# Preparing eight experts' weights in five rounds of a convolution-and-attention pipeline instead of eight

## The chip, the cores and the metric

One core of one Trainium2 chip runs the whole program. The metric is the device time of one execution in microseconds (us). The engines are TensorE (PE; PEld is its weight load), VectorE (DVE), ScalarE (ACT), GpSimd (POOL) and SyncE (SP), which only issues DMAs.

## The reference

Sixteen images of 128 channels by 16x16 go through three parts, and each part is added to its input:

```
x = x + conv(group_norm(x))         # per-image 7x7 depthwise filters, made from the image itself:
                                    # softmax keys, filters = query @ keys, 1x1 conv, layer norm, relu, 1x1 conv
t = tokens(x)                       # 256 tokens of 128 per image
t = t + attention(layer_norm(t))    # q = tanh(z); softmax(q q^T / sqrt(128)) z
t = t + moe(layer_norm(t))          # 8 experts, the best 2 per token:
   h = x @ w1[e] + b1[e]
   y = (silu(h @ wg[e] + bg[e]) * (h @ wv[e] + bv[e])) @ w2[e] + b2[e]
```

There is nothing nonlinear between `w1` and `wg`, `wv`. So the kernel multiplies them once per expert: `w1[e] @ [wg[e] | wv[e]]`, a 128x512 matrix, with the bias row added, and later sends token rows through that product.

## The kernel before, in words

The work has two halves. The first is a software pipeline over 8 pairs of images. In round i (0 to 8, loop `for i in range(rounds)` of each engine's program) seven stages work on seven pairs: n = i (group norm statistics), a = i-1 (keys and transposes of the normalised pair), b = i-2 (filters), c = i-3 (convolution by spectra, and the layer norm of its result), d = i-4 (attention), e = i-5 (router), f = i-6 (sending rows to `rows_dram`). So round 0 has only n, round 1 has n and a, round 2 has b as well, and round 6 is the first with all seven. Round 8 has no n. After round 8 a tail, written out by hand, finishes the last pairs. The second half runs 71 blocks of 128 token rows through the experts, starting at about 201 us.

Each engine executes its own list in the order written; semaphores tie them. Inside a round TensorE does: transposes of the new pair (L1204, they wait for `g_done`, which ScalarE gives with `gbuf` L627), keys (L1209), the first 1x1 conv (L1145), the filter spectrum of c (L1163), transposes for attention (L1140), filter mean (L1149), the spectrum of the features (L1095), router transposes (L1103), scores (L1170), router (L1110), filter variance (L1153), **one expert's weights (`expert_weights`, L1188)**, transposes of the keys' softmax (L1277), the group average of the means (L1283, it waits for `gn_mv_done` of VectorE L929), the convolution's inverse transform (`image`, L1178), ranks, the group average of the squares (L1296), raw filters (L1303), attention (L1132), and the last 1x1 conv (`filter_of`, L1158). `keep_busy` (L1090) puts 128x256 matmuls without use into gaps of the early rounds.

One expert x costs, by engine: VectorE `weight_differences` (L678, L679: makes `w1d`, at the end of the round before), TensorE two 128x512 matmuls into `bank_d0` (L1188), VectorE `weight_bias` (L686, adds the bias to row 0 of the bank), ScalarE the copy to `w_high` (L600 or L614), VectorE `low_part` (L692: bank minus `w_high` to `w_low`). Rounds 1 to 8 do expert i-1 each. `wgv`, `w1t` and `bg_row` are double-buffered by x % 2, and SyncE's `reload_w(x)` waits for `wmul_psum` of expert x-2 before it loads.

GpSimd computes inverse roots (L440 for the filters, L446 for group norm, L450 and L459 for the two layer norms) and issues indirect DMAs of rows (L429), all in one queue: in a round from 6 on, two rows' worth (4 DMAs) stand between L440 and L446.

Of the kernel before, what the change touches and what calls it, by code (L numbers as in the profile page):

```python
# [32 lines left out]
ALU = mybir.AluOpType  # L33
# [93 lines left out]
def build(nc, a_in, out):  # L127
# [9 lines left out]
    with ctx:  # L137
# [202 lines left out]

        expert_rounds = list(range(1, EXPERTS + 1))

        def experts_through(i):

            return sum(r <= i for r in expert_rounds)

        def expert_in(i):
            return experts_through(i) - 1 if i in expert_rounds else None

# [5 lines left out]
        with nc.Block() as block:  # L355

            @block.sync
            def _(sp):
# [35 lines left out]
                for p in range(2, PAIRS):  # L394

                    sp.wait_ge(g_done, p - 1)
                    load_x(p)
                    if p < EXPERTS - 1:
                        reload_w(p)

                    if p < 2 + PAIRS // 2:
                        sp.dma_start(xt[:, 2 * p - 4:2 * p - 2], a_in["xt"][:, 2 * p - 4:2 * p - 2]).then_inc(ld_xt[p % 2], 16)
                reload_w(EXPERTS - 1)
                sp.dma_start(w2_all[:, :], a_in["w2"]).then_inc(ld_w2, 16)
# [99 lines left out]
            def _(act):  # L504
# [45 lines left out]
                def rest_spectrum(b):  # L550
                    act.wait_ge(ghat_psum, 2 * b + 2)
                    act.activation(ghat[0:BOTH, b % 2, 2, :], bank_s1[0:BOTH, 0:2 * C], ACT.Copy).then_inc(ghat_done, 1)

                def tanh_of(d):
# [13 lines left out]
                for i in range(rounds):  # L568
                    n, a, b, c, d, e, _ = stages(i)
                    x = expert_in(i)  # L570
                    if a is not None:

                        act.wait_ge(gt_psum, a + 1)
                        after(act, fraw_psum, a - 1)
                        after(act, ghat_psum, 2 * (a - 1))
                        act.activation(gt[:, a % 2, :, :].rearrange("p h c -> p (h c)"), bank_t[:, :], ACT.Copy).then_inc(gt_done, 1)
                    if b is not None:
                        first_conv(b)
# [18 lines left out]
                    if x is not None and b is None and a is not None:  # L597

                        act.wait_ge(wbias_done, x + 1)
                        act.activation(w_high[:, x * 2 * HID:(x + 1) * 2 * HID], bank_d0[:, :], ACT.Copy).then_inc(whigh_done, 1)  # L600
                    if d is not None:
# [9 lines left out]
                    if x is not None and b is not None and a is not None:  # L611

                        act.wait_ge(wbias_done, x + 1)
                        act.activation(w_high[:, x * 2 * HID:(x + 1) * 2 * HID], bank_d0[:, :], ACT.Copy).then_inc(whigh_done, 1)  # L614
                    if a is not None:
# [39 lines left out]
            def _(dve):  # L655
# [25 lines left out]

                def weight_bias(x):

                    dve.wait_ge(wmul_psum, x + 1)
                    dve.wait_ge(ld_bg[x % 2], 16 * (x // 2 + 1))
                    dve.tensor_tensor(bank_d0[0:1, :], bank_d0[0:1, :], bg_row[:, x % 2, :], ALU.add).then_inc(wbias_done, 1)  # L686

                def low_part(x):
# [3 lines left out]
                    dve.tensor_tensor(w_low[:, columns], bank_d0[:, :], w_high[:, columns], ALU.subtract).then_inc(wlow_done, 1)  # L692

# [179 lines left out]
                for i in range(rounds):  # L873
                    n, a, b, c, d, e, _ = stages(i)
                    x = expert_in(i)
                    if i == 1:

                        dve.wait_ge(ld_c1, 32)
                        dve.tensor_copy(before[:, :], cst("before")).then_inc(const_ready, 1)
                        dve.wait_ge(ld_router, 32)  # L880
                        dve.tensor_tensor(router_d[:, :], router_w, router_0[:, :], ALU.subtract).then_inc(router_sub, 1)
                        dve.wait_ge(router_sub, 1)
                        dve.tensor_copy(router_d[0:1, :], router_b[:, :]).then_inc(router_done, 1)
                        experts["triangle"](dve)
                        image_statistics(n)
                    if b is not None:
                        centred(b)
# [13 lines left out]
                    if x is not None and b is None and a is not None:  # L901
                        weight_bias(x)
                    if c is not None:
# [34 lines left out]
                    if x is not None and a is not None:  # L938
                        if b is not None:
                            weight_bias(x)  # L940
                        low_part(x)
                    if n is not None:
# [140 lines left out]
            def _(pe):  # L1083
# [97 lines left out]

                def expert_weights(i, x):

                    pe.wait_ge(wdiff_done, x + 1)
                    after(pe, prod_done, through(i, CC))
                    after(pe, wlow_done, x)
                    for h in range(2):
                        last = pe.matmul(bank_d0[:, :], w1d[:, h, :], wgv[:, x % 2, h, :], start=(h == 0), stop=(h == 1))  # L1188
                    last.then_inc(wmul_psum, 1)

                for i in range(rounds):
                    n, a, b, c, d, e, _ = stages(i)
                    x = expert_in(i)
                    if a is not None:
# [16 lines left out]
                    if x is not None and b is None and a is not None:  # L1211
                        expert_weights(i, x)
                    if b is not None:
# [49 lines left out]
                    if b is not None:  # L1263

                        if b < 2:
                            keep_busy(bank_o[:, 0:2 * P], 3)
                        after(pe, logits_done, through(i, E))
                        filter_square(b)
                    if x is not None and b is not None and a is not None:
                        expert_weights(i, x)  # L1270
                    if a is not None:
# [582 lines left out]
```

## Time and profile before

| what | value |
|---|---|
| median of 3 runs | 332.0 us (331.98 to 333.33) |
| the profiled execution: its own time | 332.57 us |
| its span, first to last instruction | 330.6 us |
| mean granted TensorE clock | 0.969 of full |
| busy over the span | PE 90%, PEld 72%, DVE 70%, ACT 44%, POOL 50% |
| chain that ended last, by engine | PE 65%, DVE 16%, issue 6%, POOL 4%, DMA 3%, ACT 3% |

The span begins at the first instruction; 2.0 us of the execution's time lie around it. A time in the text as "at 104.45" counts from the start of the span. "Records" of TensorE are halves of a matmul here: each fp32 matmul shows as two.

### The profile page before, as it was taken

What the parts mean: (1) busy time and instruction counts of PE and PEld (TensorE: products, weight loads), DVE (VectorE), ACT (ScalarE), POOL (GpSimd) and SP (SyncE); (2) the same over time, 40 slices, a digit from 0 to 9 for tenths busy, and PEclk for the clock granted to TensorE, in tenths of its full rate; (3) what the DMA queues carried; (4) which work ended last, traced back from release to release, by engine and by line L of the source; (5) the groups of instructions that cost most, each with busy time, mean ns of one, the idle gap of its engine ahead of it and who ended that gap; (6) DMA issues with size and microseconds to landing.
All of it is one profiled execution on the core that took longest, in us unless ns stands there. A gap on an engine that the chain in (4) does not pass through costs nothing.

```text
span 330.6 us, 7141 instructions
## 1 busy us (share of the span) xinstructions
PE 296.0 (90%) x1733; PEld 236.5 (72%) x1733; DVE 232.8 (70%) x1012; ACT 144.5 (44%) x465; POOL 164.7 (50%) x187
## 2 busy tenths in 40 slices
PE   0889999999999999999998986999999999999910
PEld 0557777688777778778876764876888888888810
DVE  2424375679788797877889795688666676767883
ACT  1344343625237352461420424555566666666600
POOL 3000002021163746636748765667777777676650
PEclk9979999999999999999999998799999999999985
DMA  6751423050211811001101113334433333335937
GB/s 189 281 171 45 133 76 102 4 168 5 80 48 34 285 39 35 16 24 36 34 25 50 44 41 93 99 98 108 113 92 104 89 105 108 97 84 153 353 131 250
DMA packets 29920, 33.39 MB, mean 101 GB/s; under 512 B 5064, under 2 KB 23836, under 8 KB 29626
## 3 DMA queue, kind: packets, MB, share of 16 engines
q1 hardware_dynamic: 24608, 23.64, 24.3%
q0 software_dynamic: 4352, 8.60, 7.6%
q10 hardware_dynamic: 922, 0.71, 0.7%
q8 instruction: 16, 0.26, 0.4%
q14 instruction: 22, 0.18, 0.2%
HBM read 21.69 MB, written 11.68 MB: 101 GB/s over the span
## 4 chain that ended last, share of the span: by engine, by line
PE 65%; DVE 16%; issue 6%; POOL 4%; DMA 3%; ACT 3%; DVEq 1%; POOLq 0%; SPq 0%; ACTq 0%
PE bank L1784 7%; PE bank L1178 6%; PE bank L1095 6%; PE bank L1188 4%; PE bank L1759 4%; PE bank L1764 4%; PE bank L1760 4%; PE bank L1773 4%; PE bank L1163 3%; PE bank L1170 3%; PE bank L1090 3%; POOL rows_dram L429 3%; PE bank L1754 2%; DVE ys L1699 2%; PE bank L1132 2%
## 5 line engine op out<-in xcount | busy, mean ns | idle before, releaser
L1492 POOL DMA_INDIRECT moe_dram<-ys,xs x71 | 70.0, 987 | 29.0 <-issue 19.5
L429 POOL DMA_INDIRECT rows_dram<-row,slot x56 | 55.6, 993 | 24.6 <-issue 13.5
L1784 PE MATMUL bank<-w_all,gatedt 128*128 x284 | 44.1, 278 | 0.1
L1580 ACT ACTIVATE silu<-bank 128x256 f32<-128x256 f32 x71 | 27.2, 383 | 33.3 <-PE bank L1764 32.9
L1699 DVE SCALAR_TENSOR_TENSOR ys<-b_all,xs,bank 128x128 f32<-128x128 f32 x71 | 24.7, 348 | 23.0 <-issue 20.5
L1716 DVE SCALAR_TENSOR_TENSOR gated<-bank,xs,silu 128x256 f32<-128x256 f32 x71 | 34.2, 482 | 7.4 <-ACT silu L1580 3.4
L1784 PEld LDWEIGHTS bank<-w_all,gatedt 128*128 128x128 f32 x284 | 37.7, 193 | 0.3 <-issue 0.3
L1759 PE MATMUL bank<-w_high,x_high 128*128 x71 | 34.8, 491 | 2.6 <-ACT x_high L1567 2.6
L440 POOL TENSOR_TENSOR frstd<-fvar,minus_half 128x2 f32<-128x2 f32 x7 | 4.9, 706 | 52.4 <-DVE fvar L802 52.4
L1764 PE MATMUL bank<-w_high,x_low 128*128 x71 | 29.5, 415 | 0.4
L1178 PE MATMUL bank<-zhat,const 121*128 121x256 f32 (+1 forms) x128 | 29.6, 383 | 0.1
L1760 PE MATMUL bank<-w_low,x_high 128*128 x71 | 28.4, 400 | 0.0
L1773 PE MATMUL bank<-const,gated 128*128 128x128 f32 x142 | 27.9, 278 | 0.6 <-DVE gated L1716 0.6
L1571 ACT ACTIVATE gatedt<-bank 128x256 f32<-128x256 f32 x71 | 26.9, 379 | 1.2 <-PE bank L1773 1.1
L1773 PEld LDWEIGHTS bank<-const,gated 128*128 128x128 f32 x142 | 19.6, 142 | 9.5 <-DVE gated L1716 2.2
L1178 PEld LDWEIGHTS bank<-zhat,const 121*128 121x128 f32 (+1 forms) x128 | 23.6, 189 | 3.7 <-issue 0.5
L1567 ACT ACTIVATE x_high<-bank 128x128 fp32r<-128x128 f32 x71 | 19.7, 277 | 10.5 <-PE bank L1754 3.6
L1090 PE MATMUL bank<-const 128*128 128x256 f32 x82 | 23.5, 416 | 0.0
L1095 PE MATMUL bank<-gt,const 128*121 128x256 f32 (+1 forms) x96 | 22.8, 385 | 0.0
L1690 DVE TENSOR_TENSOR x_low<-bank,x_high 128x128 fp32r<-128x128 f32 x71 | 20.3, 286 | 3.3 <-ACT x_high L1567 3.2
L446 POOL TENSOR_TENSOR gn_rstd<-gn_var,minus_half 128x2 f32<-128x2 f32 x8 | 5.7, 715 | 32.1 <-DVE gn_var L966 32.1
L1764 PEld LDWEIGHTS bank<-w_high,x_low 128*128 128x128 f32 x71 | 13.6, 191 | 8.5 <-DVE x_low L1690 2.9
(203 smaller groups left out, 623.2 us busy)
## 6 DMA issues: line engine op xcount, KB each, us to landing
xs<-rows_dram SPq DMA_DIRECT2D x71, 66.0 KB, 1.9
xc<-in_x SPq DMA_DIRECT2D x8, 256.0 KB, 3.1
wgv<-in_wg SPq DMA_DIRECT2D x8, 256.0 KB, 2.8
wgv<-in_wv SPq DMA_DIRECT2D x8, 256.0 KB, 3.1
xt<-in_xt SPq DMA_DIRECT2D x4, 512.0 KB, 4.9
xt<-moe_dram SPq DMA_DIRECT2D x8, 256.0 KB, 4.5
moe_dram<-ys,xs POOLq DMA_INDIRECT x71, 2.3
const<-in_const SPq DMA_DIRECT2D x1, 1123.0 KB, 9.6
```

The source lines that it names most:

```text
L429: pool.indirect_dma_start(rows_dram, bass.IndirectOffsetOnAxis(ap=slot[:, f % 2, 2 * t + k:2 * t + k + 1], axis=0), row[:, f % 2, t, k, :] ...
L1090: pe.matmul(bank, ident, const[:, 0:2 * P], start=True, stop=True)
L1095: last = pe.matmul(bank_s[r // 2][0:tile_rows[r], r % 2 * 2 * C:(r % 2 + 1) * 2 * C], fwd[:, h, tile_cols[r]], gt[:, b % 2, h, :], start=( ...
L1178: last = pe.matmul(bank_o[:, h * 2 * C:(h + 1) * 2 * C], inv[0:tile_rows[r], r, h * P:(h + 1) * P], zhat[0:tile_rows[r], r, :], start=(r = ...
L1492: pool.indirect_dma_start(moe_dram, bass.IndirectOffsetOnAxis(ap=xs[:, u, C + 1:C + 2].bitcast(U32), axis=0), ys[:, u, :], None, bounds_ch ...
L1699: dve.scalar_tensor_tensor(ys[:, u, :], b2_all[:, bass.ds(e * C, C)], xs[:, u, C:C + 1], bank_y[j % 2][:, 0:C], ALU.mult, ALU.add).then_in ...
L1716: dve.scalar_tensor_tensor(gated[:, j % 2, :], bank_h[j % 2][:, HID:2 * HID], xs[:, j % U, C:C + 1], silu[:, j % 2, :], ALU.mult, ALU.mult ...
L1759: pe.matmul(bank_h[j % 2][:, :], x_high[:, j % 2, :], w_high[:, bass.ds(e * (2 * HID), 2 * HID)], start=True, stop=False)
L1760: pe.matmul(bank_h[j % 2][:, :], x_high[:, j % 2, :], w_low[:, bass.ds(e * (2 * HID), 2 * HID)], start=False, stop=False)
L1764: pe.matmul(bank_h[j % 2][:, :], x_low[:, j % 2, :], w_high[:, bass.ds(e * (2 * HID), 2 * HID)], start=False, stop=True).then_inc(S["h_psu ...
L1773: last = pe.transpose(bank_g[:, h * P:(h + 1) * P], gated[:, j % 2, h * P:(h + 1) * P], ident)
L1784: last = pe.matmul(bank_y[j % 2][:, 0:C], gatedt[:, j % 2, h * P:(h + 1) * P], w2_all[:, bass.ds(e * (2 * C) + h * C, C)], start=(h == 0), ...
```

## The change

Experts are no longer one per round. `middle_expert` says which expert is made in the old place of a round (0, 2, 4, 6, 7 in rounds 1 to 5), `late_expert` which one is made as a second one at the end of TensorE's round (1, 3, 5 in rounds 1 to 3), into `bank_o`. Rounds 6, 7 and 8 make none. The late one's bias, high copy and low part come at the start of the next round; the differences of the late expert follow `low_part` of the middle one, those of the next middle expert follow `low_part` of the late one. The loads are issued in the order in which the buffers come free. Of `keep_busy` ahead of the transposes, the counts (3, 2, 2, 4) become (3, 0, 0, 0).

```diff
-        expert_rounds = list(range(1, EXPERTS + 1))
+        middle_expert = {1: 0, 2: 2, 3: 4, 4: 6, 5: 7}
+        late_expert = {1: 1, 2: 3, 3: 5}
 SyncE:
-                    if p < EXPERTS - 1:
-                        reload_w(p)
+                    for x in {2: (2,), 3: (3, 4), 4: (5, 6), 5: (7,)}.get(p, ()):
+                        reload_w(x)
...
-                reload_w(EXPERTS - 1)
 ScalarE, after the copy to gt and before first_conv:
+                    if late_in(i - 1) is not None:
+                        high_copy(late_in(i - 1), bank_o)
 VectorE, first in the round:
+                    late = late_in(i - 1)
+                    if late is not None:
+                        weight_bias(late, bank_o)
 VectorE, after kshift (L900) and before products:
+                    if late is not None:
+                        low_part(late, bank_o)
+                        if x is not None:
+                            weight_differences(x)
 VectorE, in the middle, before gn_dev (L945):
-                        low_part(x)
+                        low_part(x, bank_d0)
+                        if late_in(i) is not None:
+                            weight_differences(late_in(i))
 VectorE, end of the round:
-                    if expert_in(i + 1) is not None:
+                    if late_in(i) is None and expert_in(i + 1) is not None:
                         weight_differences(expert_in(i + 1))
 TensorE:
-                            keep_busy(bank_t[:, 0:2 * P], (3, 2, 2, 4)[a])
+                            keep_busy(bank_t[:, 0:2 * P], (3, 0, 0, 0)[a])
...
                         if b == 0:
-                            keep_busy(bank_o[:, 0:2 * P], 1)
+                            keep_busy(bank_d1[:, 2 * P:4 * P], 1)
...
                         if b < 2:
+                            pe.wait_ge(wlow_done, late_in(i - 1) + 1)
                             keep_busy(bank_o[:, 0:2 * P], 3)
...
+                        if late_in(i - 1) is not None:
+                            pe.wait_ge(wlow_done, late_in(i - 1) + 1)
                         image(c)
...
                         filter_of(b)
+                    if late_in(i) is not None:
+                        expert_weights(i, late_in(i), bank_o)
```

## Rows read from the trace of the kernel before

**Rows 1.** Window of round 6: PE, PEld, DVE, ACT, POOL busy; clock; DMA share, GB/s.

```profile
92.95:113.50 20.55, 19.93 (x118) 15.94 (x118) 17.20 (x93) 9.16 (x31) 11.74 (x12) 1.00 0.38 111
```

**Rows 2.** The chain that ended last, round 6: start us, us, what.

```profile
103.16 0.20 DVE logits L730
...
103.79 1.82 PE bank L1188 x4
...
105.95 3.58 PE bank L1178 x16
```

**Rows 3.** Timeline of VectorE in rounds 6 and 7: start, duration, line [idle before].

```profile
98.11 1.27 DVE L723 TENSOR_SCALAR row<-t,ln_mv,ln_rstd 128x127 f32<-128x127 f32 x4 [0.31 <-POOL ln_rstd L459]
...
104.45 0.24 DVE L929 BATCH_NORM_AGGREGATE gn_mv<-gn_raw 128x2 f32<-128x6 f32 x2
...
112.06 0.16 DVE L975 SCALAR_TENSOR_TENSOR gn_bias<-gn_mean,gn_rstd 128x2 f32<-128x2 f32 x1
```

**Rows 4.** Timeline of POOL in rounds 6 and 8 and the tail.

```profile
105.16 0.72 POOL L440 TENSOR_TENSOR frstd<-fvar,minus_half 128x2 f32<-128x2 f32 x1 [4.54 <-DVE fvar L802]
...
109.95 0.95 POOL L429 DMA_INDIRECT rows_dram<-row,slot  x1 [0.30 <-issue]
110.92 0.73 POOL L446 TENSOR_TENSOR gn_rstd<-gn_var,minus_half 128x2 f32<-128x2 f32 x1
...
153.11 1.04 POOL L450 TENSOR_TENSOR ln_rstd<-ln_var,minus_half 128x4 f32<-128x4 f32 x1 [1.21 <-DVE ln_var L669]
...
172.28 1.03 POOL L429 DMA_INDIRECT rows_dram<-row,slot  x1 [3.88 <-DVE slot L789]
```

**Rows 5.** Timeline of VectorE, one pair of weight differences, start to start.

```profile
11.17 0.17 DVE L678 COPY w1d<-b1c 128x2 f32<-128x2 f32 x1 [0.93 <-DMA w1t<-in_w1t]
...
11.58 0.22 DVE L879 CAST before<-const 128x128 bf16<-128x128 f32 x1
```

**Rows 6.** Timeline of TensorE from the end of round 1 into round 2.

```profile
18.21 0.38 PE L1296 MATMUL bank<-gn_e,const 128*128 128x2 f32 x2 [0.57 <-DVE gn_e L953]
18.46 1.08 PE L1303 MATMUL bank<-pt,gt 128*128 128x64 f32 x8
19.38 1.74 PE L1090 MATMUL bank<-const 128*128 128x256 f32 x4
20.95 1.12 PE L1204 MATMUL bank<-const,gbuf 128*128 128x128 f32 x4
...
24.28 0.38 PE L1149 MATMUL bank<-fsum,const 128*128 128x2 f32 x2 [0.31 <-ACT f L534]
24.53 2.83 PE L1095 MATMUL bank<-gt,const 128*121 128x256 f32 x12
```

**Rows 7.** Windows around the low clock of round 1 (columns as in rows 1).

```profile
14.50:15.00 0.50, 0.50 (x2) 0.19 (x1) 0.00 (x0) 0.22 (x2) 0.00 (x0) 1.00 0.08 26
...
19.50:20.00 0.50, 0.50 (x3) 0.44 (x3) 0.39 (x3) 0.42 (x2) 0.08 (x1) 0.66 0.89 295
...
23.00:23.50 0.50, 0.50 (x5) 0.45 (x4) 0.00 (x0) 0.00 (x0) 0.00 (x0) 0.93 0.03 8
```

**Rows 8.** Timeline of TensorE, ends of rounds 2 and 3.

```profile
35.01 1.13 PE L1090 MATMUL bank<-const 128*128 128x256 f32 x4
36.26 0.66 PE L1204 MATMUL bank<-const,gbuf 128*128 128x128 f32 x4
...
51.52 1.99 PE L1090 MATMUL bank<-const 128*128 128x256 f32 x8
53.47 0.66 PE L1204 MATMUL bank<-const,gbuf 128*128 128x128 f32 x4
```

**Rows 9.** Timelines of ScalarE (round 3) and VectorE (rounds 3 and 4).

```profile
38.41 0.20 ACT L534 ACTIVATION_READ_ACCUMULATOR f<-bank,small 128x1 f32 x1
...
44.17 0.16 DVE L912 RECIPROCAL krec<-ktot 128x1 f32<-128x1 f32 x1 [0.92 <-ACT kexp L589]
...
64.86 0.69 DVE L686 TENSOR_TENSOR bank<-bank,bg_row 1x512 f32<-1x512 f32 x1 [1.34 <-PE bank L1188]
```

More of the change, by code:

```diff
@@ L339, in build, with late_in @@
         CC = 3
-        expert_rounds = list(range(1, EXPERTS + 1))
+        middle_expert = {1: 0, 2: 2, 3: 4, 4: 6, 5: 7}
+        late_expert = {1: 1, 2: 3, 3: 5}
         def experts_through(i):
-            return sum(r <= i for r in expert_rounds)
+            return max([x + 1 for r, x in middle_expert.items() if r <= i], default=0)
         def expert_in(i):
-            return experts_through(i) - 1 if i in expert_rounds else None
+            return middle_expert.get(i)
+        def late_in(i):
+            return late_expert.get(i)
         def after(eng, semaphore, count):
@@ L552, in rest_spectrum, with high_copy @@
                     act.activation(ghat[0:BOTH, b % 2, 2, :], bank_s1[0:BOTH, 0:2 * C], ACT.Copy).then_inc(ghat_done, 1)
+                def high_copy(x, bank):
+                    act.wait_ge(wbias_done, x + 1)
+                    act.activation(w_high[:, x * 2 * HID:(x + 1) * 2 * HID], bank[:, :], ACT.Copy).then_inc(whigh_done, 1)
                 def tanh_of(d):
@@ L597, in _ @@
                     if x is not None and b is None and a is not None:
-                        act.wait_ge(wbias_done, x + 1)
-                        act.activation(w_high[:, x * 2 * HID:(x + 1) * 2 * HID], bank_d0[:, :], ACT.Copy).then_inc(whigh_done, 1)
+                        high_copy(x, bank_d0)
                     if d is not None:
@@ L611, in _ @@
                     if x is not None and b is not None and a is not None:
-                        act.wait_ge(wbias_done, x + 1)
-                        act.activation(w_high[:, x * 2 * HID:(x + 1) * 2 * HID], bank_d0[:, :], ACT.Copy).then_inc(whigh_done, 1)
+                        high_copy(x, bank_d0)
                     if a is not None:
@@ L680, in weight_differences, with weight_bias, low_part @@
                                       w1t[:, x % 2, :, 0:1].broadcast_to([P, 2, C - 1]), ALU.subtract).then_inc(wdiff_done, 1)
-                def weight_bias(x):
+                def weight_bias(x, bank):
                     dve.wait_ge(wmul_psum, x + 1)
                     dve.wait_ge(ld_bg[x % 2], 16 * (x // 2 + 1))
-                    dve.tensor_tensor(bank_d0[0:1, :], bank_d0[0:1, :], bg_row[:, x % 2, :], ALU.add).then_inc(wbias_done, 1)
-                def low_part(x):
+                    dve.tensor_tensor(bank[0:1, :], bank[0:1, :], bg_row[:, x % 2, :], ALU.add).then_inc(wbias_done, 1)
+                def low_part(x, bank):
                     columns = slice(x * 2 * HID, (x + 1) * 2 * HID)
                     dve.wait_ge(whigh_done, x + 1)
-                    dve.tensor_tensor(w_low[:, columns], bank_d0[:, :], w_high[:, columns], ALU.subtract).then_inc(wlow_done, 1)
+                    dve.tensor_tensor(w_low[:, columns], bank[:, :], w_high[:, columns], ALU.subtract).then_inc(wlow_done, 1)
                 def products(c):
@@ L901, in _ @@
                     if x is not None and b is None and a is not None:
-                        weight_bias(x)
+                        weight_bias(x, bank_d0)
+                    if late is not None:
+                        low_part(late, bank_o)
+                        if x is not None:
+                            weight_differences(x)
                     if c is not None:
@@ L939, in _ @@
                         if b is not None:
-                            weight_bias(x)
-                        low_part(x)
+                            weight_bias(x, bank_d0)
+                        low_part(x, bank_d0)
+                        if late_in(i) is not None:
+                            weight_differences(late_in(i))
                     if n is not None:
@@ L1180, in image, with expert_weights @@
                     last.then_inc(conv_psum, 1)
-                def expert_weights(i, x):
+                def expert_weights(i, x, bank):
                     pe.wait_ge(wdiff_done, x + 1)
-                    after(pe, prod_done, through(i, CC))
-                    after(pe, wlow_done, x)
+                    if bank is bank_d0:
+                        after(pe, prod_done, through(i, CC))
+                        after(pe, wlow_done, x)
+                    else:
+                        after(pe, t1_done, through(i, CC))
+                        after(pe, wlow_done, x - 1)
                     for h in range(2):
-                        last = pe.matmul(bank_d0[:, :], w1d[:, h, :], wgv[:, x % 2, h, :], start=(h == 0), stop=(h == 1))
+                        last = pe.matmul(bank[:, :], w1d[:, h, :], wgv[:, x % 2, h, :], start=(h == 0), stop=(h == 1))
                     last.then_inc(wmul_psum, 1)
@@ L1211, in _ @@
                     if x is not None and b is None and a is not None:
-                        expert_weights(i, x)
+                        expert_weights(i, x, bank_d0)
                     if b is not None:
@@ L1269, in _ @@
                     if x is not None and b is not None and a is not None:
-                        expert_weights(i, x)
+                        expert_weights(i, x, bank_d0)
                     if a is not None:
```

## The prediction

> **What bounds the kernel now.** I read the windows by round first (rounds 7 and 8 repeat round 6 nearly), then the chain of waits, then the timelines of VectorE, POOL and TensorE where the moved steps stood and where they go. In round 6 TensorE is busy 19.93 of 20.55 us at the full clock of 2.4 GHz and VectorE 17.20 [rows 1]. The chain runs through TensorE there, the expert's 1.82 us included [rows 2]. That looks as if 1.82 us per round could be had. But inside the round TensorE meets two results of VectorE: the copied logits (L730, 103.16), and the group norm averages (L929, done at 104.45 + 0.24 = 104.69), behind which the convolution transform stands [rows 2, 3]. Today the second is hidden by the expert's matmuls. VectorE is itself held from before (L723 waited 0.31 us for POOL) [rows 3], so it will not be earlier by itself. At the end of the early rounds TensorE runs filler: 1.57 us at the end of round 1 (19.38 to 20.95) [rows 6], 1.25 us after round 2 (35.01 to 36.26) and 1.95 us after round 3 (51.52 to 53.47) [rows 8].
>
> **Late side: three experts leave rounds 6 to 8.** Round 6. Without the expert TensorE has done the variance and the softmax transposes by 104.1 (103.79, plus the 0.34 that now lie between the expert's end at 105.61 and the transform at 105.95) and waits for 104.69. The average's matmuls lie between; by L1296 and its successor (18.21 to 18.46) I give them 0.25 and the semaphore 0.1 to 0.2, so the transform starts at about 105.1 and not at 105.95 [rows 2, 3, 6]. So 0.8 of 1.82 us is won, to the nearest tenth. Gone with the expert are VectorE's bias and low part too, but they stood behind L929 and gave way to the transform anyway; they buy slack before the image's sum, no time.
> Round 7. TensorE's start is set by `gbuf`, after L975 (112.06), after POOL's L446. POOL issues four row DMAs back to back between L440 (105.16) and L446 (110.92); none of them waits for what moves, so L446 stays at 110.92 and ends at 111.65 [rows 4]. L975 moves from 112.06 to about 111.7, that is 0.36 earlier and not 0.8 [rows 3, 4]. The router and the logits inherit 0.36, L929 behind them also; then the expert's place gives 0.8 again: the transform is 1.2 early.
> Round 8. By the same chain L440 is 0.36 early in round 7 and L446 with it; L975 would be 1.2 early by VectorE, and is 0.75 early by POOL (111.65 + 20.55 - 0.36, against 132.61, the repeat of L975 one round on). Here there is no group norm, so nothing is in the way of the transform but the expert: 0.75 + 1.82 = 2.5 us early at its end. L450 (153.11) comes behind POOL's row DMAs and is only 2.0 early [rows 4], but TensorE's list in the tail is nearly full and stands 2.5 early; POOL's next long chain starts at 172.28 with a wait of 3.88 us for VectorE's slots, which come from TensorE's ranks [rows 4]. So it follows TensorE, and I carry **2.5 us** into the second half. Bounds: 1.2 (no more than the 0.75 of POOL and some, if the tail is POOL's) and 3 x 1.82 = 5.5 (if VectorE's chain is shorter than I read it).
> In the Trainium skill's "Perfetto Trace Analysis", section "GPSIMD Engine Instruction", a GpSimd duration in a profile is called unreliable, and start-to-start spacing is recommended. By the durations of L429 (four at 0.95 to 1.03) POOL would be free near 110.0 and round 7 would start 0.8 early, which would make the late side some 0.8 us more; the starts (109.95, then 110.92) say it is not free, and the sum above goes by the starts [rows 4].
>
> **Early side: three experts come to the ends of rounds 1 to 3.** Three things are added.
> The differences of the late expert now stand before L945, in the chain of group norm (VectorE, average, POOL, gbuf), instead of behind it. One pair takes 11.58 - 11.17 = 0.41 us start to start; with the semaphore I take 0.45 [rows 5]. In round 1 the data are there: the DMA share is down to 0.08 at 14.5 us [rows 7]. The later loads are issued by SP right after g_done or after the previous product of their buffer, half a round or more before their use, so no wait for DMA is added; if one were, it would sit in the same chain.
> Round 1. TensorE's L1296 moves from 18.21 to 18.66, L1303 ends at 19.85, and the late expert starts where the filler stood at 19.38. The clock granted falls to 1.2 GHz at about 19.7 (0.66 in its half microsecond) and is back at 23.05 (0.93) [rows 7]; TensorE had been idle 0.57 us before 18.21 [rows 6], and will be idle 1.0 now. At 1.2 GHz 1.82 us of matmul take 3.64. The last bit runs after the clock's return: it ends near 23.3. The transposes start there and not at 20.95, 2.35 us late. Some comes back, since now the transposes, the keys and the first conv run mostly at the low clock, 3.58 us from 20.95 to L1095 at 24.53 [rows 6]. At full clock the same takes 2.6: in round 3, 36.26 to 38.61 until ScalarE has the conv out, plus 0.25 for the mean (24.28 to 24.53) [rows 6, 8, 9]. So L1095 starts at about 25.9, **1.4 us** late. Bounds: -0.3 if the clock does not fall (19.85 + 1.82 = 21.7, and 2.6 on), 3.1 if it stays down for another 3.4 us.
> Round 2. TensorE's end of round is late by the 0.45 above. The late expert's 1.82 us stands where 1.25 us of filler and wait stood, 35.01 to 36.26 [rows 2, 8]. gbuf, also 0.45 late, is hidden under it. So 0.45 + 1.82 - 1.25 = **1.0 us**. Bounds: 0.45 and 1.3.
> Round 3. VectorE gets the low part (by L686, as wide, 0.69, some 0.6 start to start) and differences before the products, 1.05 us; it meets the wait of 0.92 us for the softmax's sum there [rows 9], so that L929 is late by 0.1 and TensorE does not see it. The second differences stand before L945, whose result TensorE wants only after the transform. The late expert needs 1.82 of 1.95 us [rows 2, 8]. **0.0**; bounds 0 and 0.5.
> Round 4 has the late low part and the differences ahead of a wait of 1.34 us [rows 9]: 0. ScalarE's copy fits between gt and the first conv, where it waits for TensorE; the late bias is done by then: 0. The second bank costs nothing by itself; its waits (`wlow_done` before the fillers and the image) are for a low part that VectorE has made right after kshift, while TensorE is still in L1095.
> The fillers that go are counted above, as what stood in the wait for gbuf; nothing else is won with them.
>
> **The sum.** Early +1.4 + 1.0 + 0.0 = +2.4; late -2.5; together -0.1 us. The profiled execution took 332.57 and would take 332.5. It is 0.57 above the median of 332.0, so the forecast as a median is **331.9 us**.
>
> **Rivals.**
> A, slower: the low clock of round 1 is prolonged. For it: the added differences lengthen the idle gap ahead of it, and fillers go. Against: the late expert keeps TensorE busy in the whole stretch. The present stretch lasts 3.4 us (19.7 to 23.05) [rows 7]. One more such stretch costs half of it, 1.7, two more 3.4, over work that is dense from 24.53 on [rows 6]. With the forecast's -0.1 that is 333.5 to 335.2, middle 334.4. It decides from 1.8 us more, a stretch of 3.6.
> By the Trainium skill ("TensorE: Matmul & The Clock Gate", section "The HAM clock gate") the clock is restricted by default and activity releases it, at moments not tied to the kernel's start. Rows 7 show one fall and one return, and no run here shows yet how they move; the page would allow A and B alike.
> B, faster: the clock doesn't fall in round 1 or only briefly, since real matmuls stand there. Round 1 is then -0.3 instead of 1.4, early +0.7: 330.2.
> C, faster: TensorE alone bounds rounds 6 to 8, as its 19.93 of 20.55 us suggests [rows 1]. Late is -5.5 and the sum -3.1: 328.9. Against it stands L929's 104.69.
> D, the move doesn't reach the end: POOL's row DMAs hold rounds 7, 8 and the tail, late is -0.8 to -1.2. Sum +1.4: 333.4.
>
> **How the numbers follow.** What a measurement of this kernel can tell from no change is about 0.5%, 1.7 us. Chances: forecast 0.42, A 0.20, B 0.16, C 0.10, D 0.12. The forecast's own range is 330.6 to 333.4. Faster by over 0.5% (under 330.3): C and most of B, and a sliver of the forecast, 0.27. Slower (over 333.7): most of A, half of D and little of the forecast, 0.25. Within: 0.48. The range for 8 in 10 is 329.6 to 334.4.
>
> **What would show it.** Right: rounds 2 and 3 begin 2 to 3 us later than 20.95 and 36.26 give; rounds 6 and 7 last 0.4 to 0.8 us less and not 1.8, with TensorE waiting for L929 and POOL's L446 directly behind an L429; the second half starts within 0.5 us of where it did. Wrong: a round 7 shorter by 1.5 us or more (C), a clock of 1.0 through 19 to 24 us (B), a low clock beyond 24 us (A), or slots in the tail that wait for POOL (D).

## The result: slower by 0.7 to 1 per cent

| | kernel before | changed kernel | ratio, 95% interval |
|---|---|---|---|
| first comparison, 20 executions each | 332.02 us median | 334.70 us median (332.63 to 336.47) | 1.0068 [1.0049, 1.0086] |
| second comparison, 29 and 6 executions | 332.29 us | 335.50 us | 1.0103 [1.0072, 1.0133] |

The forecast was 331.9 us, the range 329.6 to 334.4. The time lies above both. Gains and losses in us below are worked out from the ratio, of about 332 us: 2.3 and 3.4 us here (the differences of the medians are 2.7 and 3.2). In "331.03 against 332.29" and the like, the second number is the kernel before, timed in the same comparison.

**The profile after** is of an execution of 334.95 us (span 332.9 us, mean granted clock 0.953; before 0.969). First the windows of rounds 6 and 7, columns as in rows 1: PE, PEld, DVE, ACT, POOL busy, clock, DMA share, GB/s.

```profile
96.28:116.45 20.17, 18.43 (x113) 15.20 (x114) 16.04 (x92) 8.46 (x30) 11.54 (x12) 1.00 0.33 119
116.45:136.62 20.17, 18.43 (x113) 15.19 (x114) 15.54 (x90) 8.46 (x30) 11.37 (x12) 1.00 0.09 28
```

The expert's matmuls are gone (19.93 busy before, 18.43 now), yet the round is only 0.38 us shorter than in [rows 1]. TensorE's idle time in it rose from 0.62 to 1.74 us. Its timeline in round 6 and at the start of round 7 shows where; the last bracket is the idle time ahead of the row and who ended it.

```profile
106.98 0.42 PE L1296 MATMUL bank<-const,kprob 128*128 128x128 f32 x2
108.07 0.38 PE L1302 MATMUL bank<-gn_mv,const 128*128 128x2 f32 x2 [0.67 <-DVE gn_mv L941]
108.32 1.98 PE L1192 MATMUL bank<-zhat,const 121*128 121x256 f32 x8
...
116.45 0.63 PE L1222 MATMUL bank<-const,gbuf 128*128 128x128 f32 x4 [0.74 <-ACT gbuf L632]
```

VectorE's average (L941, L929 before) and POOL's inverse root (L449, L446 before):

```profile
107.78 0.24 DVE L941 BATCH_NORM_AGGREGATE gn_mv<-gn_raw 128x2 f32<-128x6 f32 x2
...
115.02 0.16 DVE L989 SCALAR_TENSOR_TENSOR gn_bias<-gn_mean,gn_rstd 128x2 f32<-128x2 f32 x1 [0.37 <-POOL gn_rstd L449]
```

```profile
113.28 0.96 POOL L432 DMA_INDIRECT rows_dram<-row,slot  x1 [0.30 <-issue]
114.27 0.72 POOL L449 TENSOR_TENSOR gn_rstd<-gn_var,minus_half 128x2 f32<-128x2 f32 x1
```

L941 ends 107.78 + 0.24 - 96.28 = 11.74 us into the round, as L929 did in [rows 3] (104.69 - 92.95 = 11.74). The transform starts 12.04 into it, not 13.00 [rows 2]. POOL's L449 stands directly behind the last row DMA, as L446 did in [rows 4]. Both limits that the prediction named for these rounds are there.

At the end of round 1 (to be read against [rows 6]):

```profile
18.08 0.42 PE L1317 MATMUL bank<-gn_e,const 128*128 128x2 f32 x2 [0.97 <-DVE gn_e L967]
18.36 1.95 PE L1324 MATMUL bank<-pt,gt 128*128 128x64 f32 x8
20.10 3.73 PE L1206 MATMUL bank<-wgv,w1d 128*128 128x512 f32 x4
23.62 1.06 PE L1222 MATMUL bank<-const,gbuf 128*128 128x128 f32 x4
24.61 0.89 PE L1227 MATMUL bank<-gbuf,small 128*64 128x256 f32 x4
...
26.90 0.89 PE L1109 MATMUL bank<-gt,const 128*121 128x256 f32 x3
```

The windows there, against [rows 7]:

```profile
18.00:18.50 0.50, 0.42 (x3) 0.42 (x3) 0.03 (x1) 0.00 (x0) 0.00 (x0) 0.80 1.21 234
...
21.50:22.00 0.50, 0.50 (x2) 0.08 (x1) 0.00 (x0) 0.07 (x1) 0.00 (x0) 0.50 0.00 0
...
25.00:25.50 0.50, 0.50 (x5) 0.07 (x1) 0.00 (x0) 0.50 (x2) 0.00 (x0) 0.88 0.67 143
```

The low level (0.50, 1.2 GHz) was granted for 6.8 us, from about 18.3 to 25.1, where [rows 7] has 3.4. The late expert took 3.73 us. The ends of rounds 2 and 3, against [rows 8]:

```profile
37.78 1.98 PE L1206 MATMUL bank<-wgv,w1d 128*128 128x512 f32 x4
39.60 0.60 PE L1222 MATMUL bank<-const,gbuf 128*128 128x128 f32 x4
...
54.80 1.98 PE L1206 MATMUL bank<-wgv,w1d 128*128 128x512 f32 x4
56.84 0.63 PE L1222 MATMUL bank<-const,gbuf 128*128 128x128 f32 x4
```

**One table for all profiles.** Each number is a difference of two start times in TensorE's timeline. "gn to L1109": from the group average of round 1 (L1296 before, L1317 after) to the first large spectrum of round 2 (L1095, L1109). "to round 3": from there to the transposes of round 3. "r6", "r7": length of the round. "3 to 71": from the start of round 3 to the first matmul with expert weights of the 71 blocks. "Low us" is the mean over all timed executions of the kernel of twice (1 - mean granted clock) times the span: how long an execution spent at the low level. In the profiles 15 to 21 us of it lie behind 199 us, in the second half and at the end. A "low stretch" is one stretch of about 3.4 us at the low level, and rounds 6 to 8 without their expert are called thinned.

| kernel | gn to L1109 | to round 3 | r6 | r7 | 3 to 71 | low us, mean |
|---|---|---|---|---|---|---|
| before | 6.32 | 11.73 | 20.55 | 20.54 | 165.35 | 20 |
| before_again | 6.34 | 11.73 | 20.55 | 20.54 | 165.35 | 20.4 |
| changed, first profile | 8.82 | 12.70 | 20.17 | 20.17 | 164.87 | 27.3 |
| changed, after_again | 7.20 | 12.71 | 21.40 | 21.40 | 165.66 | 27.7 |
| changed, after_look1 | 7.22 | 12.70 | 20.16 | 20.16 | 163.06 | |
| changed, after_look2 | 7.19 | 12.71 | 21.40 | 23.02 | 168.32 | |
| changed, after_look3 | 5.52 | 12.71 | 21.40 | 20.17 | 164.29 | |
| late_only | 6.32 | 11.73 | 21.40 | 20.17 | 164.80 | 22.9 |
| late_gaps | 5.38 | 11.74 | 20.09 | 20.11 | 163.07 | 19.7 |
| early_only | 7.21 | 12.70 | 20.56 | 20.56 | 165.41 | 21.4 |
| early_look | 5.52 | 12.70 | 20.55 | 20.56 | 165.28 | |
| before_fill | 5.27 | 11.73 | 20.55 | 20.55 | 165.65 | 19.4 |
| after_fill | 5.53 | 12.70 | 20.16 | 21.39 | 164.30 | 20.9 |
| after_gaps | 7.22 | 12.70 | 20.08 | 20.11 | 162.98 | 23.0 |
| diffs_later | 7.21 | 12.30 | 20.16 | 20.17 | 163.18 | 24.6 |
| six | 6.30 | 12.70 | 20.54 | 20.17 | 164.81 | 23.2 |
| after_all | 5.52 | 12.30 | 20.07 | 20.10 | 163.01 | 17.7 |
| six_best | 5.28 | 12.30 | 20.54 | 20.08 | 163.45 | 17.4 |

The group average itself starts between 17.5 and 20.2 us with no order to it; in the five profiles of the changed kernel it starts between 18.1 and 20.2. So single spans are not compared here; medians and these differences are.

### The profile page after: what moved, and what is told of

Read it like the earlier page. It is cut to its first block, busy times and chain, and to the rows that moved or that the text cites. A ratio compares the mean times of both kernels' runs of the same rounds, so it can differ in the third digit from the quotient of the medians.

```text
span 332.9 us, 7111 instructions
## 1 busy us (share of the span) xinstructions
PE 296.1 (89%) x1717; PEld 236.2 (71%) x1717; DVE 232.7 (70%) x1012; ACT 143.8 (43%) x465; POOL 163.9 (49%) x187
## 4 chain that ended last, share of the span: by engine, by line
PE 67%; DVE 14%; DMA 6%; issue 5%; POOL 3%; ACT 3%; DVEq 1%; SPq 0%; POOLq 0%; ACTq 0%
PE bank L1192 8%; PE bank L1807 7%; PE bank L1109 6%; PE bank L1206 4%; PE bank L1177 4%; PE bank L1782 4%; PE bank L1787 4%; PE bank L1783 4%; PE bank L1796 4%; PE bank L1184 3%; PE bank L1146 3%; POOL rows_dram L432 2%; PE bank L1324 2%; PE bank L1777 2%; DVE ys L1722 2%
## 5 line engine op out<-in xcount | busy, mean ns | idle before, releaser
L1603 ACT ACTIVATE silu<-bank 128x256 f32<-128x256 f32 x71 | 27.3, 384 | 33.2 <-PE bank L1787 32.8
L1192 PE MATMUL bank<-zhat,const 121*128 121x256 f32 (+1 forms) x128 | 30.3, 390 | 0.0
L1192 PEld LDWEIGHTS bank<-zhat,const 121*128 121x128 f32 (+1 forms) x128 | 24.4, 195 | 3.6 <-DVE t L857 0.2
L1590 ACT ACTIVATE x_high<-bank 128x128 fp32r<-128x128 f32 x71 | 19.7, 278 | 10.6 <-PE bank L1777 3.6
L1109 PE MATMUL bank<-gt,const 128*121 128x256 f32 (+1 forms) x96 | 22.8, 385 | 0.0
L449 POOL TENSOR_TENSOR gn_rstd<-gn_var,minus_half 128x2 f32<-128x2 f32 x8 | 5.7, 715 | 32.1 <-DVE gn_var L980 32.1
L1777 PE MATMUL bank<-const,xs 128*128 128x128 f32 x71 | 19.8, 282 | 0.0
L1104 PE MATMUL bank<-const 128*128 128x256 f32 x66 | 19.6, 425 | 0.0
```

The costliest lines, as they stand in the source:

```text
L1109: last = pe.matmul(bank_s[r // 2][0:tile_rows[r], r % 2 * 2 * C:(r % 2 + 1) * 2 * C], fwd[:, h, tile_cols[r]], gt[:, b % 2, h, :], start=( ...
L1192: last = pe.matmul(bank_o[:, h * 2 * C:(h + 1) * 2 * C], inv[0:tile_rows[r], r, h * P:(h + 1) * P], zhat[0:tile_rows[r], r, :], start=(r = ...
L1603: act.activation(silu[:, j % 2, :], bank_h[j % 2][:, 0:HID], ACT.Silu).then_inc(S["silu_done"], 1)
```

## The experiments

Theory at the start: both sides of the sum are as forecast, and the low clock takes the difference. Rival: one side was mis-sized by a wait that the forecast missed.

**1. The late part alone** (`late_only`): the kernel before without experts 5, 6 and 7 and their loads; GpSimd sets zeros in place of their products. The main line of the edit:

```diff
-        expert_rounds = list(range(1, EXPERTS + 1))
+        expert_rounds = list(range(1, 6))
```

> The kernel before, with experts 5, 6 and 7 left out: rounds 6, 7 and 8 make no expert's weights, their products are zeros set by POOL at the start; rounds 1 to 5 are as before. So it has the late side of the change alone. The prediction's theory (TensorE waits for the group norm averages L929, POOL holds L446): 2.5 us less than the kernel before, with the transform 0.8, 1.2 and 2.5 us early in rounds 6, 7, 8. The rival that TensorE alone bounds these rounds: 5.5 us less. The rival that the gain is lost behind round 8 (tail bound by POOL or by DMAs): at most 1.2 us less, although the transform of round 8 is 2.5 early.

Measured: 331.03 against 332.29 us, 0.9976 [0.9949, 1.0002], a gain of 0.8 (0 to 1.7) and not of 2.5 us. The profile is of its slowest execution (333.04 us, clock 0.953; the twelve go from 329.45). Round 7 lasted 20.17 as forecast, but round 6 21.40; a second low stretch stands at 174.1 to 177.5 us. The windows of the first, and the timeline behind them:

```profile
104.50:105.00 0.50, 0.45 (x4) 0.21 (x3) 0.47 (x8) 0.43 (x3) 0.00 (x0) 1.00 0.00 0
105.00:105.50 0.50, 0.00 (x0) 0.00 (x0) 0.50 (x9) 0.05 (x1) 0.00 (x0) 1.00 0.00 0
105.50:106.00 0.50, 0.37 (x3) 0.38 (x3) 0.50 (x8) 0.45 (x2) 0.00 (x0) 0.85 0.00 0
106.00:106.50 0.50, 0.50 (x3) 0.41 (x3) 0.50 (x6) 0.00 (x0) 0.46 (x1) 0.50 0.00 0
...
109.00:109.50 0.50, 0.50 (x3) 0.45 (x2) 0.00 (x0) 0.00 (x0) 0.27 (x1) 0.74 0.00 0
```

```profile
105.63 0.41 PE L1285 MATMUL bank<-gn_mv,const 128*128 128x2 f32 x2 [0.67 <-DVE gn_mv L931]
105.90 4.28 PE L1180 MATMUL bank<-zhat,const 121*128 121x256 f32 x11
```

TensorE stands idle for 0.67 us in the expert's old place; the granted clock falls within the next half microsecond, is at 0.50 until about 109.3, and the transform runs at half rate. A round with this stretch is 1.23 us longer than one without (21.40 against 20.17).

**2. The same with fillers in the gaps** (`late_gaps`): in rounds 6 and 7 one filler of 128x256 in each of three waits: behind the router, ahead of the wait for `gn_mv`, ahead of the wait for `gbuf`. The second of them:

```diff
+    if x is None and i >= 6:
+        keep_busy(bank_d0[:, 0:2 * P], 1)
     pe.wait_ge(gn_mv_done, n + 1)
```

> late_only (the kernel before without experts 5, 6, 7) with one filler matmul of 0.45 us each in the gaps that the missing expert left in rounds 6 and 7: after the router, before the group average of the means, and before the next round's transposes. late_only's trace has the clock at 1.2 GHz for 3.4 us in round 6 (105.5 to 109), and the round took 21.4 us; without it round 7 took 20.17. Theory: the expert's matmuls kept the clock up, and the gain of the late side is lost to the fall. Then no low clock stands in rounds 6 and 7, both take 20.2 us or less, and the kernel is 2 to 2.5 us faster than the one before and 1.2 to 1.7 faster than late_only. Rival: the falls have nothing to do with the gaps: same as late_only (0.8 us less than before), low clock in rounds 6 or 7 again.

Measured: 328.97 against 331.31 us, 0.9922 [0.9893, 0.9952]: 2.6 us, about the forecast's 2.5. Both rounds are at full clock:

```profile
91.24:111.33 20.09, 19.79 (x120) 15.97 (x120) 15.95 (x91) 8.46 (x30) 11.55 (x12) 1.00 0.33 120
111.33:131.44 20.11, 19.80 (x120) 15.98 (x120) 15.55 (x89) 8.46 (x30) 11.38 (x12) 1.00 0.09 29
```

In round 6 the wait for the group norm averages is down to 0.24 us, and the transform stands where it stood in the changed kernel, 103.28 - 91.24 = 12.04 us into the round:

```profile
103.04 0.38 PE L1292 MATMUL bank<-gn_mv,const 128*128 128x2 f32 x2 [0.24 <-DVE gn_mv L931]
103.28 3.71 PE L1180 MATMUL bank<-zhat,const 121*128 121x256 f32 x16
```

TensorE does more than in `late_only` (19.79 against the 18.43 of an undisturbed round) and is done sooner. Mean low time fell from 22.9 to 19.7 us, which at half rate is 1.6 us of time, about what was gained. The rival that the tail, bound by POOL or a DMA, takes the gain (at most 1.2 us less) would also have fitted the 0.8 of `late_only`; it does not fit 2.6. Nor do the zeros make the second half shorter: from the first block to the end `late_only` takes 129.3 us and `late_gaps` 129.4, the kernel before 129.0. Which of the three fillers is needed was not tested.

**3. The early part alone** (`early_only`): the changed kernel with four fillers in place of the missing expert in rounds 6 to 8 (TensorE's work only; VectorE's and ScalarE's part stays away).

```diff
+    if x is None and i >= 6:
+        after(pe, prod_done, through(i, CC))
+        keep_busy(bank_d0[:, 0:2 * P], 4)
```

> The changed kernel with TensorE's work put back in rounds 6 to 8: four fillers (1.8 us) where the expert's matmuls stood. So it has the early side of the change alone. Prediction's theory: 2.4 us over before with one low stretch of 3.4 us in round 1, 3.4 us over with two (rival A). If the clock's falls in rounds 6 to 8 come from the missing matmuls, none is there.

Measured: 333.62 against 331.31 us, 1.0061 [1.0034, 1.0088], 2.0 us where 2.4 were forecast. Rounds 6 and 7 are as before, with no low stretch.

**4. The changed kernel again** (`after_again`), with a timing of its own.

> The changed kernel itself once more, with a new trace. Its first trace had three things against it: the clock at 1.2 GHz for 6.7 us in rounds 1 and 2 (3.4 before), a short low clock at 175 to 178 us, and a wait of VectorE for the landing of POOL's row DMAs (L728 at 199.69) worth 1.0 us. If these belong to the change, all three are here again and the time is 2 to 3 us over before; if they are chance, one or more is missing and the span is that much shorter.

Measured: the second row of the first table. Its profile has only one low stretch in round 1, none at 175 to 178 us and no wait for a row DMA, but one low stretch in each of rounds 6 and 7. So of the three things of the first trace one was there by half and two were not, yet the span was 1.2 us longer (334.1 against 332.9) and not shorter: the cost stayed, its places moved. Three more profiles and one of the early part were taken to count them.

> The changed kernel, one more profile. If the thinned rounds are the main cause, the stretches beyond those of the kernel before lie in rounds 6, 7, 8 and the tail (a round with one lasts 21.4 us, without 20.17) and round 1 has one stretch of 3.4 us (the group average to L1109 takes 7.2 us). If the early part is, round 1 has 6.8 us of low clock (8.8 us for the same).

> The changed kernel, a second more profile. Low clock ahead of the second half: 10.2 us in all in the theory of the thinned rounds, of which 3.4 in round 1; in the other theory 6.8 of it in round 1.

> The changed kernel, a third more profile, with the same two expectations: one stretch of 3.4 us in round 1 and one or two in rounds 6 to 8 and the tail, or two in round 1.

> The early part alone (four fillers stand in place of the expert in rounds 6 to 8), one more profile. By the mean clock of its executions: one stretch of 3.4 us in round 1 and none in rounds 6 to 8, 7.2 us from the group average to L1109. Rival: 6.8 us in round 1, 8.8 us for the same stretch of work.

Measured (table; the five profiles of the changed kernel in its order): low stretches in round 1: 2, 1, 1, 1, 0; in rounds 6 and 7 together: 0, 2, 0, 3, 1. Both expectations were too orderly. The double stretch of the first profile is one of five; the early part has one or none in round 1 and none in rounds 6 and 7.

Over all 18 profiles: where round 6 or 7 is thinned and has no filler (`late_only`, the five of the changed kernel, `after_fill`, `diffs_later`, `six`), a low stretch stands in rounds 6 and 7 in 5 of 9; where the expert or fillers stand in both, in 0 of 9. The worst late one, of after_look2, as windows of its rounds 6 and 7:

```profile
94.81:116.21 21.40, 20.12 (x113) 16.34 (x114) 15.49 (x89) 8.49 (x30) 11.59 (x12) 0.92 0.31 113
116.21:139.23 23.02, 21.73 (x113) 17.61 (x114) 15.58 (x89) 8.49 (x30) 11.58 (x12) 0.85 0.08 25
```

The same 113 records as in the first profile's rows take 20.12 and 21.73 us instead of 18.43. And after_look3, where the clock did not fall in round 1 although the wait ahead is the same 0.97 us:

```profile
20.18 0.38 PE L1317 MATMUL bank<-gn_e,const 128*128 128x2 f32 x2 [0.97 <-DVE gn_e L967]
20.43 1.08 PE L1324 MATMUL bank<-pt,gt 128*128 128x64 f32 x8
21.35 1.94 PE L1206 MATMUL bank<-wgv,w1d 128*128 128x512 f32 x4
23.12 0.60 PE L1222 MATMUL bank<-const,gbuf 128*128 128x128 f32 x4
```

**5. The kernel before again** (`before_again`) and with four more fillers in round 1 (`before_fill`).

> The kernel before once more, for a second profile of it. Theory: one low clock of 3.4 us in round 1 between 19 and 24 us, none in rounds 6 and 7, round 2 starts 9.5 us behind round 1 and round 3 24.8 behind; ratio 1.000. Rival: the low clock of round 1 comes and goes from one execution to the next in this kernel too; then round 2 starts 9.0 to 9.5 and round 3 24.0 to 24.8 behind round 1, and the added cost of round 1 in the changed kernel is overstated or understated by the one profile of before.

Measured: ratio 1.000 [0.998, 1.002]; one low stretch in round 1, none in rounds 6 and 7, every column of the table within 0.02 us of the first profile. The fillers of `before_fill`, ahead of the softmax transposes and ahead of the group average of the squares:

```diff
-                            keep_busy(bank_o[:, 0:2 * P], 1)
+                            keep_busy(bank_o[:, 0:2 * P], 3)
...
-                            keep_busy(bank_o[:, 0:2 * P], (0, 1, 5)[i])
+                            keep_busy(bank_o[:, 0:2 * P], (0, 3, 5)[i])
```

> The kernel before with four more filler matmuls in round 1: two more before the softmax transposes, two more before the group average of the squares, where TensorE stood idle 0.95 and 0.57 us. Theory: the low clock in round 1 follows these gaps. Then the clock stays at 2.4 GHz through 19 to 24 us and the kernel is 1 to 1.6 us faster than before. Rival: the low clock has another cause; then it is there still, and the time is the same or 0.2 us more.

Measured: 332.47 against 332.29 us, 1.0006 [0.9981, 1.0030]. In its profile the low stretch of round 1 is gone (5.27 against 6.32), as the theory has it, but the 1 to 1.6 us are not there: in that one profile a low stretch stands at 174 to 178 us, and the mean low time over all executions is what it was.

**6. The changed kernel with single repairs.** The same four fillers (`after_fill`):

> The changed kernel with two more fillers before the softmax transposes and two more before the group average of the squares of round 1, the same four that took the low clock out of round 1 in before_fill. Theory (the low clock under the late expert of round 1 makes most of the early cost): the late expert takes 1.8 us instead of 3.5, and round 3 starts 1 to 2.5 us earlier than in the changed kernel, which is 1.3 to 2.5 us slower than this one. Rival (the work itself is the cost): no more than 0.4 us less than the changed kernel.

Measured: 330.98 against 331.31 us, 0.9985 [0.9950, 1.0019]: 2.8 or 3.9 us less than the changed kernel, by the two ratios of that, and more than the 1.3 to 2.5 forecast. The late expert took 1.94 us:

```profile
17.81 0.38 PE L1317 MATMUL bank<-gn_e,const 128*128 128x2 f32 x2
18.06 1.08 PE L1324 MATMUL bank<-pt,gt 128*128 128x64 f32 x8
18.98 1.94 PE L1206 MATMUL bank<-wgv,w1d 128*128 128x512 f32 x4
```

The gap fillers of experiment 2 in the changed kernel (`after_gaps`):

> The changed kernel with the same fillers in the gaps of rounds 6 and 7. Theory of the lost clock: 1.2 to 1.7 us less than the changed kernel, that is 0.8 to 1.5 over before. Rival: no different from the changed kernel, 2.3 to 3.4 over before.

Measured: 332.68 against 331.31 us, 1.0049 [1.0019, 1.0079]: the low stretches of rounds 6 and 7 are gone in its profile, that of round 1 is there. It is 0.6 or 1.8 us under the changed kernel, by the two ratios; its interval overlaps with that of the first, so the time alone does not show a gain. The mean low time fell from 27.4 to 23.0 us. And the late differences out of the way of group norm (`diffs_later`), in rounds 1 and 2 behind `gn_var`:

> The changed kernel, but in rounds 1 and 2 the differences of the late expert stand behind L974's gn_var (VectorE, the last step of group norm before POOL's L449) and no longer before L959. Forecast by the theory of this study: the wait of TensorE before L1317 in round 1 goes back from 0.97 to about 0.5 us, round 2 starts 0.45 earlier counted from the start of round 1, round 3 another 0.45; time 0.9 us under the changed kernel, ratio to the kernel before 1.004 to 1.006. Rival 1: the idle of 0.97 us ahead of the low clock is what makes it come early or stay twice as long; then also 1.7 us or more come back, the late expert of round 1 takes 1.8 to 2.4 us and the ratio is 1.000. Rival 2: gbuf (POOL, L449) is then late instead and only round 1 gains; 0.45 us.

Measured: 332.98 against 332.62 us, 1.0026 [0.9998, 1.0055]. The wait before the group average is 0.57 again, and "to round 3" is 12.30 instead of 12.70, so 0.4 us in each of two rounds. The ratio is below the 1.004 to 1.006 of the forecast: 1.4 or 2.6 us under the changed kernel and not 0.9, with the mean low time 3 us down. A part of rival 1 may hold too, but the intervals do not tell 1.4 from 0.8, and the late expert still ran at the low clock in the profile (3.60 us).

**7. Fewer experts moved** (`six`): middle 0, 1, 3, 5, 6, 7 in rounds 1 to 6, late 2 and 4 in rounds 2 and 3.

```diff
-        middle_expert = {1: 0, 2: 2, 3: 4, 4: 6, 5: 7}
-        late_expert = {1: 1, 2: 3, 3: 5}
+        middle_expert = {1: 0, 2: 1, 3: 3, 4: 5, 5: 6, 6: 7}
+        late_expert = {2: 2, 3: 4}
```

> The changed kernel with its experts spread over six rounds instead of five: one in round 1, two in rounds 2 and 3, one in rounds 4, 5 and 6, none in rounds 7 and 8. Nothing is added to round 1. Theory (round 1's addition costs most, by the clock): the low clock lasts 3.4 us as before, early side +1.0, late side -2.2, so 1.2 us less than before and 3 to 3.5 less than the changed kernel. Rival (the early cost is in rounds 2 and 3, or behind round 8): not better than before, 0 to 1 us more.

Measured: 332.17 against 332.29 us, 1.0008 [0.9980, 1.0036], no gain where 1.2 us was forecast: round 1 is as before, round 2 pays 0.97, and of the late gain 0.5 us is there in the profile. Its way from the start of round 8 to the first block is 1.3 us longer than in `six_best` below (67.41 against 66.15), 0.9 of it by a wait for a row DMA (last section) and 0.4 by a low clock that begins at 200.3.

**8. All repairs together**, in the changed kernel (`after_all`) and in the one with six rounds (`six_best`).

> The changed kernel with three repairs together: the later differences in rounds 1 and 2, four fillers of 128x256 more in round 1 (two ahead of the transposes of the softmax, two behind the group average), and one filler in each of three waits of rounds 6 and 7. Theory: the repairs act on different losses and add: 330.98 (with the round 1 fillers alone) less 0.9 (differences) less 0.8 to 1.7 (a low clock in round 6 or 7 in about half of the executions or more) gives 328.4 to 329.3, ratio to the kernel before 0.991 to 0.994; rounds 6 and 7 last 20.1 us each, the late expert of round 1 takes 1.8 to 2.0 us and round 2 starts 9.8 us behind round 1. Rival: the fillers only shift where the low clock falls, and it falls as often elsewhere; then 330.5 to 331.3, ratio 0.998 to 1.001.

> Experts in the places: middle 0, 1, 3, 5, 6, 7 in rounds 1 to 6, late 2 and 4 in rounds 2 and 3; the same three repairs. Only two experts leave late rounds (7 and 8), none is added to round 1. Theory by the sums: early 0.55 (round 2, with the later differences) and 0.0 (round 3); late 0.4 less (round 6 keeps its expert: its 0.8 is lost, and of the rest 0.36 + 0.8 + 0.6 stay, at least 1.7 by round 8); together 1.1 to 1.9 us under the kernel before, ratio 0.994 to 0.997. Rival: as in the run with six rounds and no repair, the low clock or a landing DMA in the tail takes the gain: ratio 1.000.

Measured: `after_all` 330.02 against 332.62 us, 0.9921 [0.9895, 0.9948], from 329.23 to 330.68 in six executions; `six_best` 330.45, 0.9946 [0.9920, 0.9971]. Both beat the kernel before and the changed one, and both ratios lie in their forecasts (0.991 to 0.994 and 0.994 to 0.997); the time of `after_all` was forecast at 328.4 to 329.3, beside a kernel before that took 1.3 us less in that comparison. Round 6 of it, in windows:

```profile
93.04:113.11 20.07, 19.78 (x119) 15.97 (x119) 15.93 (x91) 8.45 (x30) 11.53 (x12) 1.00 0.34 120
```

## Why the prediction was wrong

Point by point, first what held.

- **Late steps in the rounds.** Forecast and measured in the first profile, counted from the start of round 6: start of round 7 -0.36 and -0.38, start of round 8 -0.75 and -0.75, the transform's place in round 8 -2.5 and -2.51 (147.58 - 96.28 against 146.76 - 92.95). TensorE waits for L941, POOL's L449 stands behind its row DMA. So rival C (late side -5.5) is out. At full clock the 2.5 us also reach the 71 blocks: "3 to 71" is shorter by 2.3 in after_look1 and after_gaps has 2.4.
- **Rounds 2 and 3.** +1.0 forecast, 12.70 - 11.73 = +0.97 measured; 0.0 forecast for round 3, and round 3 to round 6 lasts 56.7 us in every profile.
- **Round 1 for a given clock.** The wait ahead of the group average is 0.40 longer (0.97 - 0.57; forecast 0.45). With one low stretch L1109 is then 0.89 + 0.40 = 1.3 late (forecast 1.4), with none -0.4 (forecast -0.3), with two 2.9 (rival A's bound 3.1).

**The step that failed** is the term "I carry **2.5 us** into the second half". It took the clock of 1.00 in [rows 1] as given for rounds 6 to 8 and the tail, and priced the clock in round 1 only. But the expert's 1.8 us of matmuls was what TensorE did during the wait for L929. With them gone it idles 0.67 us there and 0.74 us at the next round's start, and in three of the five profiles of the changed kernel the clock fell in round 6 or 7, which made the round 1.2 us longer, and 2.9 where it fell twice (23.02 against 20.17). The mean of "3 to 71" over the five is 165.24 us against 165.35: of 2.5 us, 0.1 is left, below the lower bound of 1.2.

Against the undisturbed profile (after_look1, 163.06) the mean loss is 2.2 us: 1.6 in rounds 6 and 7 and 0.6 behind them. The first profile has all of its loss behind them: its rounds 6 and 7 ran at full clock, but from the start of round 8 to the first block it takes 67.85 us where after_look1 takes 66.07. It waited for a row DMA there (last section) and had a low stretch:

```profile
175.00:175.50 0.50, 0.50 (x5) 0.50 (x6) 0.49 (x2) 0.00 (x0) 0.50 (x1) 0.81 0.29 93
175.50:176.00 0.50, 0.50 (x2) 0.41 (x3) 0.50 (x2) 0.00 (x0) 0.20 (x2) 0.50 0.00 0
...
178.50:179.00 0.50, 0.50 (x3) 0.46 (x2) 0.50 (x8) 0.00 (x0) 0.50 (x1) 0.78 0.40 135
```

The stretch at this place cannot be laid to the thinned rounds, for `before_fill` has it too.

In place of the forecast's sum stands, as means over the five profiles: wait ahead of the group average +0.4, gn to L1109 +0.9 (7.19 against 6.32), to round 3 +1.0, late -0.1, together +2.1 us (0.40 + 0.87 + 0.97 - 0.11). The two comparisons say 2.3 and 3.4.

Of the rivals, A has the time (333.5 to 335.2, middle 334.4; it takes the -0.1 off twice, 333.6 to 335.3 would be its sum) and the cause, a low clock that lasts longer, but the wrong place: it had the stretch of round 1 prolonged, which is so in the first profile and in none of the other four. Who reads the first profile alone would call A right. D (333.4) had POOL hold the tail, and POOL's slots came 2.2 us early in the first profile (173.38 - 96.28 against 172.28 - 92.95).

That it is the clock and not a missed wait is shown by the pair of experiments 1 and 2: more work in the same waits, and the gain goes from 0.8 to 2.6 us.

In the Trainium skill's "TensorE: Matmul & The Clock Gate", section "The HAM clock gate", the clock is restricted by default and activity releases it, at moments not tied to the kernel's start. The five profiles of one kernel agree: the same list with the same waits has its low stretches at different places, none to three of them in rounds 6 and 7. The prediction drew on that sentence for round 1 and did not ask it of rounds 6 to 8.

**What stays open.** The mean low time of the changed kernel (27.4 us) is 7 us above that of before; the late part alone adds 3 and the early part alone 1.4. That leaves 3 us, at half rate some 1.5 us of time, which would come only with both parts together. But single executions scatter by 3 to 5.5 us about these means, so the 3 us are themselves uncertain by about 2. The fillers of round 1 take 6.5 us of low time away (`after_fill`, 20.9), where round 1 holds 3.4 us on average. Whether and why what happens in round 1 bears on how often the clock falls later was not shown. And of the repairs in `after_all` the share of each was not separated beyond experiment 6.

## What to carry to other kernels

Before work is taken out of a stage, look at what it covers: an engine that is 97% busy may be filling a wait for another engine, and what is left is that wait. On TensorE such a wait can cost twice, since the clock may fall for the matmuls behind it (here in 5 of 9 profiles, for 1.2 us or more); so price the clock where work leaves as well as where it arrives, and try a filler in the gap (here it brought 1.8 us, experiments 1 and 2). And since the low stretches come in some executions only, one profile shows one draw: compare the mean granted clock over all timed executions.

## What was not expected of the hardware

- A wait of TensorE of 0.67 us, in a round in which it is otherwise nearly always busy, was followed by 3.4 us at 1.2 GHz in one execution and by none in another of the same kernel (experiments 1 and 4).
- With four fillers that took the fall out of round 1, the kernel before was no faster; its one profile had a fall at 174 us instead (experiment 5).
- Twice in 18 profiles (the changed kernel's first, and `six`) VectorE's row copy in the tail waited for a row DMA to land, 0.95 and 0.88 us, and TensorE's transposes behind it started about as much later (TensorE idle ahead of L1117 for 1.31 us, in after_look1 for 0.31). The row is from the changed kernel:

```profile
199.69 1.11 DVE L728 TENSOR_SCALAR row<-t,ln_mv,ln_rstd 128x127 f32<-128x127 f32 x4 [0.95 <-DMA rows_dram<-row,slot]
```
